# Full attention: the row-maximum scores over 64 stacked rows, in two 64-row tiles of TensorE

## The reference, cut to what matters

```python
q = (hidden_states @ Wq.T + bq).reshape(b, s, HEADS, HEAD_DIM)
k = (hidden_states @ Wk.T + bk).reshape(b, s, HEADS, HEAD_DIM)
v = (hidden_states @ Wv.T + bv).reshape(b, s, HEADS, HEAD_DIM)
q = q * SCALE
scores = jnp.einsum('bqhd,bkhd->bhqk', q, k)
probs = jax.nn.softmax(scores.astype(jnp.float32), axis=-1).astype(scores.dtype)
out = jnp.einsum('bhqk,bkhd->bqhd', probs, v).reshape(b, s, d)
return out @ Wo.T + bo
```

## Time and profile before

| | |
|---|---|
| median of 3 runs | 3652.19 us (3649.19 to 3654.99) |
| span of the profiled execution, first to last instruction | 3648.4 us |
| full attention, first to last score matmul | about 372 to 1150 us of the span |
| TensorE clock granted, mean over the span | 0.915 of full speed |

### The profile page before, as it was taken

The page is one execution under the profiler, slowest core; times in us unless marked ns, Lnnn a source line. Parts: engine busy times, 40 slices in busy tenths (PEclk is TensorE's granted clock), DMA queues, the critical chain, the costliest instruction groups (busy, mean ns, idle before and its releaser), DMA issues. The chain is left out here.

```text
span 3648.4 us, 55901 instructions
## 1 busy us (share of the span) xinstructions
PE 2793.5 (77%) x12554; PEld 1301.0 (36%) x12555; DVE 2494.0 (68%) x4119; ACT 1822.6 (50%) x3518; POOL 374.9 (10%) x612
## 2 busy tenths in 40 slices
PE   4695899999996798699999999783834555554374
PEld 3442233333332444255555555372621101101352
DVE  5666777777774667666666666454348999999622
ACT  1113577777775102244444444301216999999121
POOL 1014000000001113000000000103042000000303
PEclk9798899999998698799999999995969999999587
DMA  6003111111112005321122112280112111110012
GB/s 187 1 0 92 41 52 47 50 52 47 50 52 77 26 0 179 123 64 62 62 64 63 64 61 68 62 166 28 43 45 84 32 32 33 33 33 18 16 44 67
DMA packets 162391, 211.87 MB, mean 58 GB/s; under 512 B 35344, under 2 KB 89872, under 8 KB 161872
## 3 DMA queue, kind: packets, MB, share of 16 engines
q1 hardware_dynamic: 158224, 202.65, 18.4%
q0 software_dynamic: 4096, 8.40, 0.8%
HBM read 124.08 MB, written 86.38 MB: 58 GB/s over the span
## 5 line engine op out<-in xcount | busy, mean ns | idle before, releaser
L1068 ACT ACTIVATE prob<-ps 128x512 f32<-128x512 f32 (+3 forms) x1792 | 903.7, 551 | 572.5 <-PE ps L978 304.3
L1118 DVE TENSOR_REDUCE neg_max<-ps 128x1 f32<-128x1024 f32 (+7 forms) x1024 | 991.0, 989 | 177.6 <-PE ps L969 157.3
L1001 PE MATMUL ps<-prob,v 128*32 128x512 f32 (+3 forms) x3584 | 830.9, 567 | 1.3 <-ACT prob L1068 1.3
L1545 DVE TENSOR_REDUCE neg_max<-ps 128x1 f32<-128x1024 f32 x512 | 579.3, 1380 | 6.3 <-PE ps L1528 6.3
L978 PE MATMUL ps<-q_stack,k_stack 128*128 128x512 bf16 (+3 forms) x1792 | 560.8, 362 | 17.8 <-ACT prob L1068 9.9
L1568 ACT ACTIVATE ps<-ps,neg_max 128x1024 f32<-128x1024 f32 x512 | 557.1, 1088 | 10.6 <-DVE neg_max L1545 10.6
L1528 PE MATMUL ps<-k_stack,q_stack 128*128 128x512 bf16 x1024 | 311.1, 386 | 285.0 <-ACT ps L1568 266.6
L969 PE MATMUL ps<-k_stack,q_stack 72*128 72x512 bf16 (+3 forms) x1792 | 455.2, 364 | 57.2 <-DMA v<-v_heads 47.5
L1001 PEld LDWEIGHTS ps<-prob,v 128*32 128x32 f32 (+1 forms) x3584 | 340.6, 171 | 216.8 <-issue 189.6
L1116 DVE TENSOR_TENSOR ps<-ps,mask_qk 128x128 f32<-128x128 f32 x512 | 149.8, 293 | 257.7 <-PE ps L969 257.5
L978 PEld LDWEIGHTS ps<-q_stack,k_stack 128*128 128x128 bf16 x1792 | 154.4, 97 | 453.7 <-ACT prob L1068 353.3
(11 more groups left out here) (246 smaller groups left out, 2733.6 us busy)
## 6 DMA issues: line engine op xcount, KB each, us to landing
q_stack<-q_parts SPq DMA_DIRECT2D x576, 48.0 KB
k_stack<-k_parts SPq DMA_DIRECT2D x576, 48.0 KB
o_wide<-o_out SPq DMA_DIRECT2D x64, 260.0 KB
o_quads<-o_out SPq DMA_DIRECT2D x64, 256.0 KB
v_heads<-v_out SPq DMA_DIRECT2D x4, 4096.0 KB
v<-v_heads SPq DMA_DIRECT2D x64, 256.0 KB
num<-o_wide SPq DMA_DIRECT2D x16, 1024.0 KB
q_parts<-parts SPq DMA_DIRECT2D x24, 384.0 KB
```

Source lines behind the costliest of these rows:

```text
L1001: nc.tensor.matmul(out, vs[j.slot(4)][:, :, kt], prob[:, n % RING, o:GROUP], start=start, stop=stop).then_inc(pv_mm.sem, 1)
L1068: nc.scalar.activation(prob[:, m % RING, o:GROUP], ps[:, S2 + m % 2, o:GROUP], ACT.Exp).then_inc(exped.sem, 1)
L1118: nc.vector.tensor_reduce(neg_max[:, i.slot(2), qt:qt + 1], ps[:, bank:bank + 2, :].rearrange("p b n -> p (b n)")[:, 0:keys], AX.X, ALU.ma ...
L1545: nc.vector.tensor_reduce(neg_max[:, i.slot(2), qt:qt + 1], ps[:, 2 * (qt % 4):2 * (qt % 4) + 2, :], AX.XY, ALU.max, negate=True).then_inc ...
```

## The change

For the full attention the first pass no longer contracts rows 0 to 71 for both key halves. It leaves out the last eight rows of the nine products (the product of the two smallest parts, in the scores for the maximum alone) and contracts 64 rows (`HALF`). The first key half uses rows 0 to 63 of the stacks. The second uses rows 64 to 127 of two new buffers, `q_low` and `k_low`, which hold a copy of rows 0 to 63; so the two matmuls lie on two different 64-row tiles of TensorE. The copies are made by two more DMAs a head, SBUF to SBUF, 64 partitions of 2048 bytes each. SP issues them in `double` at the end of its step, after a wait for the head's whole load, and TensorE waits for both at the start of the step that needs them. The second pass, and the causal attention, stay as they are.

```diff
+HALF = (PARTS * PARTS - 1) * HD
...
+        q_low = [] if causal else [sb(f"q_low{n}", [P, SEQ], BF16) for n in range(2)]
+        k_low = [] if causal else [sb(f"k_low{n}", [P, SEQ], BF16) for n in range(2)]
...
+        doubled = [sem(f"doubled{n}") for n in range(2)]
...
                     q, k = qs[i.slot(4)], ks[i.slot(4)]
+                    if not causal:
+                        low, own = slice(HALF, P), slice(0, HALF)
+                        nc.tensor.matmul(ps[:, bank, :], q[own, qt * P:(qt + 1) * P], k[own, 0:GROUP],
+                                         start=True, stop=True)
+                        nc.tensor.matmul(ps[:, bank + 1, :], q_low[i.slot(2)][low, qt * P:(qt + 1) * P],
+                                         k_low[i.slot(2)][low, GROUP:SEQ], start=True, stop=True).then_inc(s1_mm.sem, 1)
+                        return
                     for c in range(CH):
-                        n = min(GROUP, (qt + 1) * P - c * GROUP) if causal else GROUP
+                        n = min(GROUP, (qt + 1) * P - c * GROUP)
...
                     if one:
                         pe.wait_ge(loaded[i.slot(4)], (i.rounds(4) + 1) * LOADS)
+                        if not causal:
+                            pe.wait_ge(doubled[i.slot(2)], (i.rounds(2) + 1) * 32)
...
+                def double(i, n):
+                    slot, low = i.slot(4), i.slot(2)
+                    sp.wait_ge(loaded[slot], (i.rounds(4) + 1) * LOADS)
+                    if n in (2, 3):
+                        s1_mm.wait(sp, i.times(KTS, -KTS - 1))
+                    for dst, src in ((q_low[low], qs[slot]), (k_low[low], ks[slot])):
+                        sp.dma_start(dst[HALF:P, :], src[0:HALF, :]).then_inc(doubled[low], 16)
+
                 def step(i, n):
...
                         sp.dma_start(qs[h.slot(4)][STACK:STACK + SHIFT, :].rearrange("r (q t) -> r q t", t=P),
                                      shift_rows[MP:MP + SHIFT * KTS, h.slot(2), :]).then_inc(shifted[h.slot(2)], 16)
+                    if not causal and (n is None or n + 1 < HEADS):
+                        double(i - (-1), None if n is None else n + 1)
 
                 load(Head(0, 0), 0)
+                if not causal:
+                    double(Head(0, 0), 0)
                 run(sp, step)
```

## The result

The change made the kernel slower: 3764.01 us (3757.34 to 3773.41, 4 runs) against 3650.69 us (3647.1 to 3654.99, 4 runs) in the same comparison, ratio 1.0313, 95% interval 1.0294 to 1.0332. The span of the profiled execution is 3767.0 us, 118.6 more than before. The forecast was 3745 us in a range of 3705 to 3805, and slower with a chance of 0.91.

What follows compares the result with a forecast made beforehand. The prediction took ScalarE's loop to bound the kernel before and SP's load, wait and copies after: 60 steps x 1.5 us = 90, plus 2.9 at the start, +93 us, so 3745 us, range 3705 to 3805.

Steps and rivals of the forecast that it cites:

- the loop through ScalarE: Second-pass matmuls, two exponentials, next weight load and `weigh` in full attention: said to set the group's 2.99 us.
- a TensorE bound: Rival: first pass on the path in every group, row tiles save 110 us, giving 3542 us; chance 0.04.
- the slack: Room between the first-pass matmuls and ScalarE's part of the loop in one group: about 0.12 us.
- A change of tiling: On TensorE, switching to or from row tiles in a group: 0.1 us each, two per group, 0 for the step.
- tiles that don't overlap: First pass in each group: +0.1 us or more past the slack; rival with costly changes 3799 us, chance 0.05.
- a loop through SP: Step start, `weigh`, load, wait, copies, step start: said to set a 13.4 us step against 11.90, 60 times.
- step start to `v`'s issue: First part of SP's loop: 7.58 us, with the slot freed 0.13 us sooner.
- `v`'s issue to the first copy's: Load landing on SP's queue, 2.99 us, plus 0.4 us from the end of the wait to SP's first DMA.
- first copy's issue to the second's: On SP's queue: 0.35 us for the issue and 0.1 between, 0.45 us.
- second copy's issue to TensorE: Landing of the copy before TensorE's next step: 2.1 us, between 1.6 and 2.95.
- The rival in which a gap brings back the half clock: A 1.5 us TensorE gap each step halves its clock: step 17.8 us, +357 us, 4009 us; chance 0.04.
- The start: The very first step of full attention starts later by its own copies, 0.4 + 0.45 + 2.1 = 2.9 us.

Runs made afterwards that it cites:

- run 2: The changed kernel with copies for heads 0 and 1 only, later heads reusing those for the second key half's maxima: 3643.19 us, ratio 0.9974 to the kernel before.
- run 4: The kernel before with 64 rows contracted, both key halves on the first 64-row tile, no copies: 3687.18 us, ratio 1.0092 to the kernel before.
- run 1: The changed kernel with both copies and both waits kept, but the first pass again 72 rows: 3770.57 us, ratio 1.0313 to the kernel before.
- run 3: The changed kernel with TensorE's wait for the copies moved right before the first pass that reads them: 3642.39 us, ratio 0.9974 to the kernel before.
- run 6: The changed kernel with SP's wait and both copies right after the load, before the store and maxima: 3811.98 us, ratio 1.0446 to the kernel before.
- run 5: The changed kernel with six needless matmuls on TensorE before its wait for the copies, from head 4 on: 3777.57 us, ratio 1.0341 to the kernel before.
- run 11: The changed kernel with late copy wait, a third PSUM bank for second scores, and the maxima's transpose behind the third group's `weigh`: 3623.86 us, ratio 0.9926.

## Why the prediction was right, point by point

**TensorE isn't the bound; the loop through ScalarE holds the group.** Right. The tiles do all that they could, two matmuls in the time of one, and alone they bring 10 us (run 2) where a TensorE bound would have given 110. The 10 us were missed: I read the slack in one group and put 0 for the step, while the group with the transpose had none. The term was 0 and measured 0.15 us a step (10 us over 64 heads).

**A change of tiling costs 0.1 us.** Right, 0.10 to 0.11 in run 4. My bound for tiles that don't overlap, 0.1 us a group or more past the slack, came out as 0.15 for a plain group (3.07 against 2.92 us), 0.13 in the mean (34 us over 256 groups).

**The copies close a loop through SP, and it sets the step.** Right, and shown from three sides: the copies alone give the whole loss (run 1), the tiles alone none of it (run 2), and the loop cut at TensorE's wait takes it all back with every DMA still made (run 3). Run 6 adds that the copies wait for the load and not for the queue. One sign was forecast wrongly: SP's queue was to be hardly idle afterwards, and it waits 3.7 us a step for `weigh`.

**The size of the step.** 13.4 us was forecast and 13.9 measured, so +93 us where it was +113 (3764.01 - 3650.69). By terms, averaged over 55 steps of the timeline of the changed kernel:

| term | forecast | measured |
|---|---|---|
| step start to `v`'s issue | 7.58 - 0.13 = 7.45 | 7.83 |
| `v`'s issue to the first copy's | 2.99 + 0.4 = 3.39 | 3.01 |
| first copy's issue to the second's | 0.45 | 0.60 |
| second copy's issue to TensorE | 2.10 | 2.49 |
| step | 13.39 | 13.93 |

The first and the last term were 0.4 us too small, the third 0.15, and the second 0.4 too long. For the last I put the landing near the floor of a lone store's packets; a copy of 64 partitions inside SBUF took 2.3 us to land and 2.35 to 2.56 us from issue to TensorE's start. The estimate of 2.3 us from the Trainium skill, "DMA: Bandwidth & Descriptors", Anatomy of one DMA, is what the trace shows for the landing, though the page fitted it on the other issuing path. The first term is off because one step stood for all (7.64 on average before, 7.58 in mine) and because of the clock, 0.15 to 0.3 us (run 5). The second was too long because I counted the waiter's reaction twice: in the first head of the changed kernel the copy goes 3.03 us after `v` (369.97 to 373.00), where TensorE started 2.99 us after it before. In the steps that time runs from 2.1 to 3.9 us, and why isn't shown; that its mean, 3.01, is so near to the first head's is partly luck. So is the closeness of the sum: the errors of the first two terms, 0.38 us each way, cancel.

**The clock.** The rival in which a gap brings back the half clock was held at 0.04 as a state for the whole stretch. What happened lies between: single drops, 0.96 of full speed over the stretch, worth 9 to 17 us (run 5).

**The start.** 2.9 us was forecast; the first matmul came 3.6 us later (376.04 against 372.41 in the earlier trace rows). Of this 0.55 us was there before the copies (`v`'s issue at 369.97 against 369.42), so the copies cost 3.1. By the start of step 4 the lag is down to 1.8 us (418.70 against 416.89). The steps between have less work for TensorE and run partly at the low clock; what share each had isn't shown.

Still open: what the time would be with the late maxima of run 11 issued sooner, and why a load takes 2.1 us to land in one step and 3.9 in another.

## What to carry to other kernels

Where an in-order queue issues a transfer and then another that depends on it, and an engine's wait closes the loop, sum issue, landing, issue and landing from step start to step start: here the second pair cost 2 us a step. Put the wait at the first instruction that reads the data, behind the work that lets the next load go; here this took all of it back. A TensorE that showed 710.75 of 711 us busy was no bound while its weight loads stood idle for another engine: halving the time of its first pass brought 10 us, not 110. Look for the loop that takes the whole period before paying for a faster matmul, and after each gain look again: with the third bank and the tiles a new wait was the DMA with the maxima.

## What the runs showed of the hardware

Two matmuls of 64 rows and 512 columns on the two row tiles start within 0.01 us of each other, and the next pair follows 0.23 us later, against 0.215 us for a single one of 72 rows. The weight loads of the two also run together (0.09 us each, started within 0.01 us). A change between 64-row tiles and the full array cost 0.10 to 0.11 us each way (run 4).

In the changed kernel the granted clock fell from 2.4 to 1.2 GHz for short stretches, 0.96 of full speed in the mean of 420 to 1240 us. It did so in 18 of 58 steps, after TensorE had stood 1.7 to 3.1 us at the step start; 40 other steps, after 0.8 to 2.7 us, show no fall. `weigh` took 1.94 us in such a step, 1.09 in another. Where the gap was partly filled (run 5), or was gone (run 3), the clock stayed at 1.00.

An SBUF to SBUF copy of 64 partitions of 2048 bytes landed 2.3 us after its issue in the median and kept SP's queue for 0.56 to 0.59 us; a store of 128 such rows to DRAM kept it for 0.35.
